# A two-layer audio tower on one core: the second layer's last pair is finished in two half steps, filling products wait for scatters, two bias loads move behind weights

## What is computed

```python
h = tok(x)                                   # conv of stride 2, LayerNorm with gamma and beta
h = h + window_attention(layernorm(h))       # 16 heads of 16, window 64
h = h + moe0(layernorm(h))                   # 16 experts (256 -> 352 -> 256), top 2, a capacity, a shared expert
h = h + causal_attention(layernorm(h))       # 16 heads of 16
h = h + moe1(layernorm(h))

def moe1(x):                                 # the part that the change is about
    logits = x @ gate_w + gate_b             # 64 experts
    top_l, top_i = top_k(logits, 3)
    gates = softmax(top_l)
    pos = rank of each (token, choice) within its expert, in order of tokens   # a running count
    buf[expert, pos] = x[token]              # at most 128 rows an expert
    y = gelu(buf @ w1 + b1) @ w2 + b2        # 256 -> 1024 -> 256
    out[token] += gate * y[expert, pos]
```

## Time and profile before

| | |
|---|---|
| median of 3 runs | 1089.98 us (1085.86 to 1090.37) |
| profiled execution | 1092.27 us, span 1090.3 us |
| busy TensorE, weight loads, VectorE, ScalarE, GpSimd | 95%, 82%, 47%, 46%, 26% |
| mean granted TensorE clock | 0.979 |
| bytes moved by DMA | 221.39 MB, mean 203 GB/s |

### The profile page before, as it was taken

One profiled execution on the slowest core, in us unless ns is written; L12 is line 12 of the kernel. 1 busy time (PEld: TensorE's weight loads), 2 busy tenths in 40 slices (PEclk: granted clock), 3 DMA queues, 4 the chain that ended last, 5 costly groups with the idle time before them and its releaser, 6 DMA issues.

```text
span 1090.3 us, 23997 instructions
## 1 busy us (share of the span) xinstructions
PE 1032.2 (95%) x7502; PEld 889.5 (82%) x7502; DVE 516.4 (47%) x2694; ACT 501.4 (46%) x1838; POOL 280.8 (26%) x324
## 2 busy tenths in 40 slices
PE   8999999899998999998985799999999999999996
PEld 7788887777776778776764789999999999999995
DVE  4878887545553456788885222222222222222221
ACT  1999999311111118998982032333333233323331
POOL 2111334502332230114254412122221222221222
PEclk9999999899998999999998899999999999999998
DMA  9954001145674440067011299999999999999990
GB/s 331 397 199 146 22 27 41 59 109 152 176 189 124 129 162 12 1 257 282 22 33 38 62 375 320 325 322 324 315 313 320 314 331 311 309 319 322 327 292 10
DMA packets 185576, 221.39 MB, mean 203 GB/s; under 512 B 64834, under 2 KB 150938, under 8 KB 184977
## 3 DMA queue, kind: packets, MB, share of 16 engines
q1 hardware_dynamic: 170384, 207.22, 56.9%
q0 software_dynamic: 15104, 13.13, 4.7%
HBM read 186.83 MB, written 44.79 MB: 212 GB/s over the span
## 4 chain that ended last, share of the span: by engine, by line
PE 80%; ACT 6%; issue 4%; DVE 4%; DMA 3%; POOL 1%; another core or an unknown queue 1%; SPq 1%; POOLq 0%; DVEq 0%; ACTq 0%
PE bank L1105 20%; PE bank L1122 19%; PE bank L964 6%; PE bank L818 4%; ACT probs L1190 4%; PE bank L850 4%; PE bank L983 3%; PE bank L938 3%; PE bank L864 2%; PE bank L827 2%; PE bank L885 2%; PE bank L841 2%; PE bank L794 2%; PE bank L800 2%; PE bank L967 2%
## 5 line engine op out<-in xcount | busy, mean ns | idle before, releaser
L1328 ACT ACTIVATE dhidT<-bank,b1T 128x128 f32<-128x128 f32 x512 | 145.8, 368 | 306.7 <-PE bank L1105 306.7
L1105 PE MATMUL bank<-probsT,arena 128*128 128x128 f32 x2048 | 239.3, 275 | 0.5 <-DVE probsT L1914 0.5
L1105 PEld LDWEIGHTS bank<-probsT,arena 128*128 128x128 f32 x2048 | 236.4, 192 | 2.5 <-DVE probsT L1914 0.8
L1122 PE MATMUL bank<-arena,dhidT 128*128 128x256 f32 x1024 | 231.6, 379 | 0.0
L1122 PEld LDWEIGHTS bank<-arena,dhidT 128*128 128x128 f32 x1024 | 189.7, 190 | 23.1
L1190 ACT ACTIVATE probs<-probs,neg_max 128x128 f32<-128x128 f32 x512 | 198.0, 395 | 4.0 <-DVE neg_max L1451 3.5
L766 POOL DMA_INDIRECT out<-probsT,slot_token x64 | 98.9, 1546 | 369.4 <-DMA out<-probsT,slot_token 272.3
L1932 DVE TENSOR_TENSOR probsT<-bank,b_wide 128x256 f32<-128x256 f32 x64 | 27.2, 425 | 340.3 <-PE bank L1122 330.0
L1451 DVE CUSTOM_DVE_ANT_0 probs<-bank,mask 128x128 f32<-128x128 f32 x512 | 115.0, 283 | 27.4 <-PE bank L841 25.3
L1190 ACT ACTIVATION_READ_ACCUMULATOR probs<-probs,neg_max 128x1 f32 x512 | 100.0, 195 | 0.0
L715 POOL DMA_INDIRECT rows<-ffn_in,scatter_i x80 | 80.5, 1006 | 40.4 <-issue 20.6
(11 more groups left out here) (167 smaller groups left out, 1380.9 us busy)
## 6 DMA issues: line engine op xcount, KB each, us to landing
arena<-L_ffn_w SPq DMA_DIRECT2D x128, 1024.0 KB, 7.9
rows<-zeros SPq DMA_DIRECT2D x13, 1024.0 KB, 10.5
arena<-L_ffn_w_gate_up SPq DMA_DIRECT2D x16, 704.0 KB
early<-rows SPq DMA_DIRECT2D x64, 80.0 KB
drows<-rows SPq DMA_DIRECT2D x32, 132.0 KB, 7.2
early<-x SPq DMA_DIRECT2D x8, 512.0 KB, 6.4
arena<-L_ffn_w_down SPq DMA_DIRECT2D x16, 256.0 KB
results<-zeros SPq DMA_DIRECT2D x4, 1024.0 KB, 12.0
```

What stands on the lines that cost most here:

```text
L1105: mm = pe.matmul(bank[2 + 2 * (u % 2) + half][:, jj * P:(jj + 1) * P], w1_sb[u][:, c, j * P:(j + 1) * P], drowsT[:, u % 2, c, :], start=c ...
L1122: last_ = pe.matmul(bank[6 + u % 2][:, 0:D], dhidT[:, u % 2, j, :], w2_sb[u][:, j, :], start=j == 0, stop=j == J1 - 1)
L1328: last_ = act.activation(dhidT[:, u % 2, j, :], bank[2 + 2 * (u % 2) + half][:, jj * P:(jj + 1) * P], ACT.Gelu, bias=b1T[:, j, bass.ds(e, 1)])
```

## The change

- `span(L, i)` gives the blocks that a step works on: both, save in the second layer from step 7 on: step 7 has block 0 of pair 7, step 8 its block 1. `pair_of` gives the pair. `STEPS1` is 9. Everything from `turn_inverse` and `normalise` to `place` and `scatter` takes its blocks from `span`; in L1 it runs nine times. What goes before `normalise` (scores, exponentials, turned probabilities, values) is left by blocks as it was. Step 7 waits for the values of block 0 alone.
- `keep_warm(52)` goes. After the last count come 3 waits with 4, 12 and 8 filling products.
- The bias parts 2 and 3 are loaded in the first turn of the expert loop, behind the loads for the experts 5 and 7.
- The lists of all five engines and `JOB_ORDER` are written anew, in both layers: the same steps in another order, with those of step 8 added. A `settle` (an empty instruction in loops) of `ln_scale` goes.

```diff
+        STEPS1 = PAIRS + 1
+        def span(L, i):
+            return (i - PAIRS + 1, i - PAIRS + 2) if L is L1 and i >= PAIRS - 1 else (0, 2)
+        def pair_of(L, i):
+            return min(i, PAIRS - 1) if L is L1 else i
...
             for p in range(PAIRS):
-                wait_read(sp, L1, (p, OUT))
+                wait_read(sp, L1, *((i, OUT) for i in range(STEPS1) if pair_of(L1, i) == p))
...
-            sp.wait_ge(L1.ffn_ready, PAIRS)
+            sp.wait_ge(L1.ffn_ready, STEPS1)
             sp.wait_ge(h_final, 16 * PAIRS)
-            load_b2(2)
-            load_b2(3)
...
                     load_w1(e + RING1, u, False)
                     load_dr(e + RING1, u, False)
                     load_w2(e + RING1, u, False)
+                    if first and u % 2 == 1:
+                        load_b2(2 + u // 2)
...
             def normalise(L, i):
-                dve.wait_ge(L.pv_done, 2 * i + 2)
+                a, b = span(L, i)
+                dve.wait_ge(L.pv_done, 2 * pair_of(L, i) + b)
                 wait_read(dve, L, (i, INVERSE))
                 wait_written(dve, L, (i - 1, OUT))
-                dve.tensor_tensor(mixedT[:, :, :], mix_bank[:, :].rearrange("p (c n) -> p c n", c=DC),
-                                  inv_rows[:, :, :], ALU.mult).then_inc(L.mix_done, 1)
+                dve.tensor_tensor(mixedT[:, :, a * P:b * P], mix_bank[:, :].rearrange("p (c n) -> p c n", c=DC)[:, :, a * P:b * P],
+                                  inv_rows[:, :, a * P:b * P], ALU.mult).then_inc(L.mix_done, 1)
```

The same a and b stand in `turn_inverse`, `project_out`, `turn_ffn_in`, `route`, `count`, `keep_inverse`, `keep_ffn_inT`, `router_exp`, `ln_scale`, `ln_stats`, `ln_moments`, `ln_apply`, `residual`, the steps from `take_logits` to `place`, and `scatter`. The end of TensorE's list:

```diff
-            turn_inverse(L1, 7); values(L1, 7, 1); project_out(L1, 7); count(L1, 6); keep_warm(4); turn_ffn_in(L1, 7)
-            route(L1, 7); count(L1, 7); keep_warm(52)
+            turn_probs(L1, 7, 0, 0); turn_probs(L1, 7, 0, 2); turn_ffn_in(L1, 6); turn_probs(L1, 7, 0, 3); count(L1, 5)
+            route(L1, 6); turn_inverse(L1, 7); values(L1, 7, 0); project_out(L1, 7); turn_probs(L1, 7, 1, 0)
+            turn_probs(L1, 7, 1, 1); count(L1, 6); turn_ffn_in(L1, 7); turn_probs(L1, 7, 1, 3); route(L1, 7)
+            turn_probs(L1, 7, 1, 2); turn_inverse(L1, 8); values(L1, 7, 1); project_out(L1, 8); keep_warm(3); turn_ffn_in(L1, 8)
+            count(L1, 7); route(L1, 8); count(L1, 8);
+
+            pe.wait_ge(L1.scatter_ready, STEPS1)
+            keep_warm(4)
+            for s, n in ((STEPS1 - 2, 12), (STEPS1 - 1, 8)):
+                pe.wait_ge(L1.scattered[s % BUFS], 16 * K1 * sum(len(range(*span(L1, i))) for i in range(s % BUFS, STEPS1, BUFS)))
+                keep_warm(n)
```

The end of ScalarE's list, and that of GpSimd:

```diff
+            keep_turned(L1, 7, 0, 2); keep_ffn_inT(L1, 6); keep_inverse(L1, 7); exponentials(L1, 7, 1, 0)
+            exponentials(L1, 7, 1, 1); exponentials(L1, 7, 1, 2); router_exp(L1, 6); exponentials(L1, 7, 1, 3)
+            keep_turned(L1, 7, 1, 0); keep_turned(L1, 7, 1, 1); keep_ffn_inT(L1, 7); keep_inverse(L1, 8); router_exp(L1, 7)
+            keep_ffn_inT(L1, 8); router_exp(L1, 8)
...
+            scatter(L1, 5, 1); scatter(L1, 5, 2); scatter(L1, 5, 3); scatter(L1, 5, 4); scatter(L1, 5, 5); ln_scale(L1, 1, 7)
+            widen(L1, 7, 1); scatter(L1, 6, 0); scatter(L1, 6, 1); scatter(L1, 6, 2); scatter(L1, 6, 3); ln_scale(L1, 1, 8)
+            scatter(L1, 6, 4); scatter(L1, 7, 0); scatter(L1, 6, 5); scatter(L1, 7, 1); scatter(L1, 8, 0); scatter(L1, 7, 2)
+            scatter(L1, 8, 1); scatter(L1, 8, 2)
```

In VectorE's list the place of step 6 comes ahead of the last turned probabilities of block 1:

```diff
+            carry(L1, 6); number_slots(L1, 6); place(L1, 6); keep_turned_dve(L1, 7, 1, 3); keep_turned_dve(L1, 7, 1, 2)
+            take_logits(L1, 7); top_values(L1, 7); top_indices(L1, 7); normalise(L1, 8); less_greatest(L1, 7)
+            mark_chosen(L1, 7); sum_pair(7); sum_weights(L1, 7); residual(L1, 8); sum_chosen(L1, 7); add_chosen(L1, 7)
+            residual_stats(L1, 8); residual_moments(L1, 8); add_to_running(L1, 7); invert_sum(L1, 7); weigh(L1, 7)
+            rank_chosen(L1, 7); take_ranks(L1, 7); expert_input(L1, 7); carry(L1, 7); expert_input(L1, 8); number_slots(L1, 7)
+            place(L1, 7); take_logits(L1, 8); top_values(L1, 8); top_indices(L1, 8); mark_chosen(L1, 8); less_greatest(L1, 8)
+            sum_pair(8); sum_chosen(L1, 8); sum_weights(L1, 8); add_chosen(L1, 8); invert_sum(L1, 8); add_to_running(L1, 8)
+            weigh(L1, 8); rank_chosen(L1, 8); take_ranks(L1, 8); number_slots(L1, 8); carry(L1, 8); place(L1, 8)
```

More of the change, by code:

```diff
@@ L882, in project_out @@
                 bk, full = new_job(L, i, OUT)
-                for t in range(2):
+                for t in range(*span(L, i)):
                     for c in range(DC):
@@ L902, in turn_ffn_in @@
                 for c in range(DC):
[L903 to L904 removed]
+                    for t in range(*span(L, i)):
+                        rows = (ffn_in[:, i % BUFS, t, c * P:(c + 1) * P] if L is L0 else
+                                h[:, 2 * pair_of(L, i) + t, c * P:(c + 1) * P])
                         last = pe.transpose(bk[:, (2 * c + t) * P:(2 * c + t + 1) * P], rows, ident[:, :])
@@ new lines, in _ @@
+            turn_probs(L1, 6, 0, 1); project_qk(L1, 7, 1); turn_probs(L1, 6, 0, 3); project_out(L1, 5); route(L1, 4)
+            project_qk(L1, 7, 0); turn_probs(L1, 6, 0, 0); scores(L1, 7, 0); count(L1, 4); turn_ffn_in(L1, 5); values(L1, 6, 0)
+            turn_probs(L1, 6, 1, 0); turn_probs(L1, 6, 1, 2); turn_probs(L1, 6, 1, 3); turn_probs(L1, 6, 1, 1); scores(L1, 7, 1)
+            route(L1, 5); turn_inverse(L1, 6); values(L1, 6, 1); turn_probs(L1, 7, 0, 1); project_v(L1, 7); project_out(L1, 6)
@@ L1359, in ln_stats @@
                 settle(dve, i)
-                for t in range(2):
+                for t in range(*(span(L, i) if w == 1 else (0, 2))):
                     last = dve.bn_stats(stats[:, w, t, :], src(t))
```

888 lines of the change are left out of this document (449 added, 439 removed).

## The result

The change made the kernel **slower by 0.8%**: 1097.66 us (median of 18 runs, 1090.71 to 1101.71) against 1088.91 us (18 runs), a ratio of 1.0081 with a 95% interval of 1.0067 to 1.0095. The forecast was 1078.0 us, range 1066 to 1090, with 6% for slower. The profiled execution of the changed kernel took 1097.38 us (span 1095.7, clock 0.976), that of before 1092.27.

What follows compares the result with a forecast made beforehand. Bound by TensorE and ScalarE before the second layer's experts, TensorE in their loop, and between them a 49.5 us stretch ended by twelve scatters. 1092.27 - 14.1 + 2.0 = 1080.2 profiled, 1078 as median; range 1066 to 1090.

Steps and rivals of the forecast that it cites:

- Orders anew at no cost, so the last values end at 586.2: All engines' lists, both layers: taken as 0, bounds a gain or loss of 5 us; last values still end near 586.2.
- The marker that I named for it: Sign in the profile: if stages before 572 us moved by over 5 us, the orders decided, not the split.
- Second half ready when the first is: Last pair, second layer: values(7,1) still ends near 586.2 if its exponentials are not late; added TensorE work costed at nothing.
- My second rival: Last pair: second half's exponentials late on ScalarE; if 8 us, gain shrinks to 6, 1084 to 1086; 0.32 with first rival.
- the marker (exponentials of half 1 later than 580): Sign in the profile, listed as wrong for the forecast: exponentials of the last pair's second half come later than 580 us.
- The pause behind the last values: Unexplained idle before the last pair's normalise: taken as gone, 5.7 us of the 14.4 us earlier last scatter.
- My first rival: The unexplained wait comes again at values of the last half or one like it: 1084; chance 0.32 with second rival.
- From the last values to the last scatter, 15.0 us: Tail before the expert loop: values end near 586.2, last scatter over at 601.2 instead of 615.64, 14.4 us earlier.
- Fill, last scatter to first turn, 6.2 us: TensorE filling behind scatters, 24 records at half clock: loop starts at 607.4, bounds 604.7 and 609.3, 14.1 us earlier.
- Bias loads, +2.0 us: Expert loop, rows of experts 6 and 8: new stall 3.2 us, old 1.18 at expert 4 gone, net 2.0 us lost.
- The third rival: Expert loop: routed rows starve behind biases, 8.7 us late twice plus half clock, 1098 us; chance 0.06.

Runs made afterwards that it cites:

- e5: Kernel before with only slots_b(7) and slots_b(8) moved ahead of hidden_b(5, 2) on VectorE, where the changed kernel has them; ratio 1.0091.
- e8: The changed kernel itself, unedited, measured again on chip C against the kernel before; ratio 1.0091.
- e7: Kernel before with only its 52 idle products replaced by the changed kernel's 4, 12 and 8 behind waits; ratio 0.9999.
- e10: e6 with the exponentials of the last pair's second half moved earlier on ScalarE, ahead of keep_inverse(7); ratio 0.9975 to the kernel before.
- e9: e6 without the split: last pair finished as one step of 256 tokens, other orders kept; ratio 0.9989 to the kernel before.
- e3: Changed kernel with the two bias loads back ahead of the expert loop; ratio 1.0020 to the kernel before.
- e1: Changed kernel with only slots_b(8) moved behind hidden_b(6, 0) on VectorE; ratio 0.9953 to the kernel before.
- e6: Changed kernel with slots_b(8) behind hidden_b(6, 0) and the two bias loads back ahead of the loop; ratio 0.9942 to the kernel before.
- e4: Kernel before with only the two bias loads moved into the expert loop's first turn; ratio 1.0028.
- e13: Kernel before with the changed kernel's orders, slots_b(8) later, for first layer, its experts and first four shared pairs; the rest old; ratio 0.9931.
- e14: Kernel before's first part with the changed kernel's second layer, split and fill, biases ahead of the loop; ratio 0.9980 to the kernel before.
- e15: Changed kernel with only slots_b(8) moved later, on chip D; ratio 0.9967 to the kernel before.

## Why the prediction was wrong, step by step

The forecast for the profiled execution was 1080.2 us, measured 1097.38: 17.2 too little. By its steps:

- **Orders anew at no cost, so the last values end at 586.2.** This step failed, and it decides the case. They ended at 599.9, 13.8 us later than before. 6.3 of it was there at the first scores of the layer: `slots_b(8)` ahead of its data, 8.0 (e5) to 14.9 us, less what the rest of the first part's orders gained. I had given the orders 0, bounds of 5 and one chance in ten of more, without reading where the moved waits stood against the loads that they wait for. The marker that I named for it, stages before 572 moved by over 5 us, came true. The wait could be read in the diff and its due time in SyncE's loop.
- **Second half ready when the first is.** The other 7.5 us arise in the second layer: about 6 on the chips without pauses (165.4 us from first scores to last values in e8, 159.7 in e7). My second rival has this in part: exponentials behind `keep_ffn_inT(6)` and `keep_inverse(7)`; the marker (exponentials of half 1 later than 580) came true, they ended at 593.5. I gave it 1084 to 1086, 6 to 8 us over the forecast. The size was right, but it came on top of the orders and the biases, and the mechanism lacked VectorE, whose copies behind the place of step 6 hold the second half when the exponentials are early (e10). It belongs to the step that failed: it is a cost of the orders and not of the halves (e9).
- **The pause behind the last values** (5.7 us between record and semaphore before) did shrink, to 2.55 us. But TensorE paused in the same way earlier, at 562 and 574 (last section). My first rival had it recurring; it moved.
- **From the last values to the last scatter, 15.0 us.** It took 18.1 here and 15.4 in e8, where no pause falls in it: right.
- **Fill, last scatter to first turn, 6.2 us.** Measured 4.85. The waits put the clock to half as said: 40 records took 6.29 us, against 4.6 at full clock (116 ns each), and the granted clock was 0.50 in the two us before 620 and 1.00 in those behind. The forecast had 24 records at the half clock, the trace has 15. In e7 the waits cost 2.5 us at the first product. The Trainium skill, TensorE: Matmul & The Clock Gate, section Why this matters for your kernels, advises against idle gaps between bursts of matmuls, since the clock goes back to half; the runs agree.
- **Bias loads, +2.0 us.** Measured +4.3 in the loop against before, 5.7 against the old place under the same fill (e3). The term was mis-sized: the rows of expert 6 were in time, those of expert 8 late by 3.49 us, close to the 3.2 taken; but the half clock behind a gap (5.46 us instead of 3.74) was left out of the sum, and so was the gain of a place ahead of the loop that with the new fill costs nothing at expert 4 (e3: no wait there). The rows of expert 8 were issued at 661.76, behind the 2176 KB of 656.58 and 1024 KB of weights; TensorE was free for them at 670.6 and got them at 674.09. The Trainium skill, DMA: Bandwidth & Descriptors, section Queues, rings and completion order, has it that each DMA engine takes the descriptors of a ring in their order; the trace agrees.
- **The third rival** gave 1098, almost the time measured, by 8.7 us of lateness twice. It was one wait of 3.49: the number came out by chance, the sign by another mechanism. (Its 5.6 us of half clock are 5.4 by its own rows, 592.57 to 598; nothing hangs on it.)

Of 17.2 us, 13.7 are the last values, 3.1 the longer tail with its pause, -1.4 the fill, +2.3 the biases, less 0.5 of rounding and of what lies outside TensorE. The range ended at 1090 because lists of several hundred reordered operations were priced like an edit with a single answer.

## What to carry to other kernels

When a diff reorders in-order queues, look up for each moved operation that waits for a transfer when that transfer can be issued at the earliest, and what stands behind it in its queue: one group, six operations too early in its list (against e1), cost 8 to 15 us at the next stage, about the whole gain that the change was to bring (12). Try a restructuring and the new orders that come with it apart: cutting the last item in two took 6.4 us off the tail (e6 against e9), and the orders written around it cost 6.5 ahead of it, with the cut and without. And a load that is moved from an idle stretch into a loop with a DMA share near 1 is paid twice, as a gap and as the half clock behind it (3.49 us, and 5.46 instead of 3.74).

## What the runs showed of the hardware

TensorE pauses inside bursts of small products with no wait on them. In the changed kernel, timeline of TensorE at `values(6, 0)`, 32 products that take 1.08 us elsewhere:

```profile
560.44 0.98 PE L875 MATMUL bank<-probsT,v_pad 128*32 128x128 f32 x16
562.53 0.38 PE L875 MATMUL bank<-probsT,v_pad 128*32 128x128 f32 x3 [1.10 <-issue]
563.99 0.42 PE L875 MATMUL bank<-probsT,v_pad 128*32 128x128 f32 x4 [1.08 <-issue]
565.44 0.82 PE L875 MATMUL bank<-probsT,v_pad 128*32 128x128 f32 x9 [1.03 <-issue]
```

The same products in e8, the same program on chip C:

```profile
554.18 1.08 PE L875 MATMUL bank<-probsT,v_pad 128*32 128x128 f32 x32
```

In e1 and e3 (chip A) the pause is at the same products (550.4 to 556.3 and 561.3 to 567.2 us), in the kernel before and in e4 at others, and on chips B, C and D there is none of this kind (two gaps of at most 0.5 us in e5 and in e7, one in e13 and in e14). So it goes with the place in the instruction stream and with the chip. The 5.7 us that looked unexplained before the change go with the same chips: ahead of that `project_out` TensorE waited 6.45 us in the kernel before and 6.66 in e4, but 1.16 or 1.17 in e5, e7 and e13, which have the same order there. The DMA view of the stretch 556 to 567 shows one transfer on each of two instruction queues; e8 has the same two from 550 to 560 and no pause. So these transfers alone do not make it, and whether TensorE waited for its instructions was not tried and stays open. Where it pauses the kernel before is 30 us (3%) slower in all than on the other chips, of which these gaps explain only a part. The first part of one and the same list also differs between executions: on chip D the first scores stood at 399.2 in e15 and at 395.7 in e13.
